# A recurrence and a mixture of experts on one core: head order, a rounded bias pass, gate transposes moved, last chunk cut 384+128

## Chip, cores and metric

One core of a Trainium2 chip. The metric is the device time of one execution in microseconds; before the change three runs gave 110.6 (median), 109.71 and 113.1.

## What is computed

From the reference, cut to what matters (x is 32 x 32 x 128, that is 32 sequences of T=32 steps; H = I = 128, E = 16 experts, K = 4 chosen):

```python
xw = einsum('ntd,dh->nth', x, Wx) + b
h_t = tanh(xw_t + h_{t-1} @ Wh)                      # scan over T
xn = h * rsqrt(mean(h*h, -1) + EPS) * norm_scale     # 1024 tokens
logits = xn @ wg + bg
vals, idx = top_k(logits, 4);  gates = softmax(vals) # spread to gate_full [token, 16]
hh = einsum('th,ehd->etd', xn, w1) + b1
a = minimum(hh[..., ::2], 7);  g = clip(hh[..., 1::2], -7, 7)
s = a * sigmoid(1.702 * a) * (g + 1)
y = einsum('eti,eih->eth', s, w2) + b2
out = x + h + einsum('eth,te->th', y, gate_full)
```

Every expert is computed for every token; the gate matrix is zero where an expert wasn't chosen. The term of b2 is therefore one matmul per token block, gates (16 per token) times b2 (16 x 128).

## The kernel before

Everything lies transposed: features on the 128 partitions, tokens as columns, 8 tiles of 128 tokens (a tile is four steps of the recurrence, 32 sequences wide). The tokens go in three chunks of 2, 2 and 4 tiles. A **unit** is 512 columns of up, activation and down work: two experts of a 2-tile chunk, or one expert of the 4-tile chunk. So chunk 0 is units 0 to 7, chunk 1 units 8 to 15, chunk 2 units 16 to 31.

The order of each engine's instructions is written out by hand, and engines meet at semaphores. The loop variable `v` counts units:

- **PE** (lines 821 to 881). First the *head*: five dummy matmuls of 512 columns on constants (`keep_warm`), then the eight steps of tiles 0 and 1. Behind steps 0, 1, 2, 4 and 6 stand two dummies of 256 columns each, behind the others useful small work; behind step 7 the rstd transpose of tile 0 (`lay_rstd(0)`), `x_wx(2)` and one more dummy. Then sums of squares of tile 1, raw logits of tiles 0 and 1, `lay_rstd(1)`, `x_wx(3, 2)`. Then units: `up` for half a (psA) and half b (psB), each as three passes in rounded fp32 (high·high, low·high, high·low; L774), one recurrence step in either slot, and `down(v - 4)` in plain fp32 (L804). An fp32 matmul shows in the trace as two instructions, a rounded one as one.
- **ACT**: relu (L483) and the gated activation (L492) of each unit in place in PSUM, tanh (L441), the high parts of w1 (L449), squares (L454), and `copy_gates` (L458). It is a queue in order: what stands behind a wait waits too.
- **DVE**: `lin` (L667), `act` (L682), norm and routing of each pair of tiles (q = 0 to 3), ending with the scale of the gates (L609).
- **POOL**: low parts of w1, powers, and the product with the gates (L406) two units behind.
- **SP**: weight loads, and for each pair the gates to DRAM and back as columns broadcast over partitions (L314, L320).

The gates of pair q are transposed by PE in unit v = 1, 7, 11 and 15 (`GATES_T`), ahead of `down(v - 4)`; ACT copies the 16 rows to `gT`. The bias of b2 starts each chunk's sum in PSUM: one fp32 matmul with 16 rows of weights per bank (L796) ahead of the first down of the chunk. The last chunk's sum lies in two banks, 256 columns in psR and 256 in psM. At the end the last four units' downs are issued bank by bank (`down_half`), each bank followed by a DVE add and a store.

## Time and profile before

| | |
|---|---|
| three runs | 110.6 us median (109.71 to 113.1) |
| the profiled execution | 110.22 us, of which the span is 108.4 us |
| busy, share of the span | PE 95%, DVE 60%, POOL 59%, ACT 56% |
| matmul instructions on PE | 562 |

The span goes from the first to the last instruction. Times in the rows are microseconds from the span's start unless a row says otherwise. In the chain view each piece is the start, the length and the work on the path that ended last. In the timeline a row may merge instructions (`x6`), and a bracket tells how long the engine was idle before it and what ended that. A matmul's record includes the time in which its last columns drain, so records overlap; the spacing of starts tells the rate.

### The profile page before, as it was taken

What the parts mean: (1) busy time and instruction counts of PE and PEld (TensorE: products, weight loads), DVE (VectorE), ACT (ScalarE), POOL (GpSimd) and SP (SyncE); (2) the same over time, 40 slices, a digit from 0 to 9 for tenths busy, and PEclk for the clock granted to TensorE, in tenths of its full rate; (3) what the DMA queues carried; (4) which work ended last, traced back from release to release, by engine and by line L of the source; (5) the groups of instructions that cost most, each with busy time, mean ns of one, the idle gap of its engine ahead of it and who ended that gap; (6) DMA issues with size and microseconds to landing.
All of it is one profiled execution on the core that took longest, in us unless ns stands there. A gap on an engine that the chain in (4) does not pass through costs nothing.

```text
span 108.4 us, 1718 instructions
## 1 busy us (share of the span) xinstructions
PE 102.9 (95%) x562; PEld 87.0 (80%) x562; DVE 64.6 (60%) x173; ACT 60.8 (56%) x139; POOL 63.8 (59%) x76
## 2 busy tenths in 40 slices
PE   7899999999999999999999969999999999999980
PEld 2557689988899999999989958886888888888760
DVE  0101367876818976399747996578266656666730
ACT  5144826899646486767716645665364566645400
POOL 3004348987791996449980799896444466545400
PEclk9999999999999999999999999999999999999999
DMA  2997930007930002991058814991000000000012
GB/s 77 235 335 266 398 113 0 0 6 234 390 159 3 0 0 74 296 379 39 12 165 246 308 60 116 336 361 59 6 0 0 0 3 0 0 0 0 0 48 48
DMA packets 4936, 12.94 MB, mean 119 GB/s; under 512 B 752, under 2 KB 1728, under 8 KB 4928
## 3 DMA queue, kind: packets, MB, share of 16 engines
q1 hardware_dynamic: 4704, 12.67, 34.7%
q10 hardware_dynamic: 224, 0.17, 0.6%
q8 instruction: 4, 0.07, 0.2%
q14 instruction: 4, 0.03, 0.1%
HBM read 12.25 MB, written 0.59 MB: 118 GB/s over the span
## 4 chain that ended last, share of the span: by engine, by line
PE 79%; DVE 9%; ACT 5%; DMA 2%; issue 1%; DVEq 0%
PE psA L774 19%; PE psB L774 17%; PE psY L804 10%; PE psR L804 5%; PE psR L722 5%; PE psM L804 5%; PE psY L722 2%; DMA wx_x_sb<-in_wx_x 2%; PE psA L751 2%; PE psM L729 2%; PE psR L714 2%; ACT psA L483 2%; PE psR L816 2%; ACT psA L492 2%; PE psM L816 2%; DVE lin L667 1%
## 5 line engine op out<-in xcount | busy, mean ns | idle before, releaser
L406 POOL TENSOR_TENSOR actg<-act,gate_cols 128x512 f32<-128x512 f32 x31 | 39.4, 1279 | 13.7 <-DVE act L682 12.9
L667 DVE TENSOR_SCALAR lin<-psB,one_b1b 128x256 f32<-128x256 f32 (+1 forms) x48 | 26.0, 569 | 23.3 <-PE psB L774 23.3
L483 ACT ACTIVATE psA<-psA,lim_b1a 128x256 f32<-128x256 f32 (+1 forms) x48 | 23.8, 515 | 26.5 <-PE psA L774 26.5
L682 DVE SCALAR_TENSOR_TENSOR act<-lin,psA 128x512 f32<-128x512 f32 x32 | 21.9, 686 | 1.8 <-ACT psA L492 0.5
L492 ACT ACTIVATE psA<-psA,limit_col 128x512 f32<-128x512 f32 x32 | 21.1, 660 | 0.8
L774 PE MATMUL psA<-xn_hi,w_hi 128*128 128x256 f32 (+1 forms) x48 | 20.5, 428 | 0.0
L804 PE MATMUL psY<-actg,w_sb 128*128 128x256 f32 x64 | 17.1, 389 | 0.0
L774 PE MATMUL psB<-xn_hi,w_hi 128*128 128x256 f32 (+1 forms) x48 | 16.0, 332 | 0.0
L774 PE MATMUL psA<-xn_hi,w_lo 128*128 128x256 f32 (+1 forms) x48 | 15.8, 328 | 0.0
L774 PE MATMUL psB<-xn_lo,w_hi 128*128 128x256 f32 (+1 forms) x48 | 15.6, 325 | 0.0
L774 PE MATMUL psB<-xn_hi,w_lo 128*128 128x256 f32 (+1 forms) x48 | 15.5, 323 | 0.0
L774 PE MATMUL psA<-xn_lo,w_hi 128*128 128x256 f32 (+1 forms) x48 | 15.5, 327 | 0.0
L389 POOL TENSOR_TENSOR w_lo<-w_sb,w_hi 128x256 fp32r<-128x256 f32 x13 | 9.2, 733 | 8.2 <-ACT w_hi L449 8.2
L804 PEld LDWEIGHTS psY<-actg,w_sb 128*128 128x128 f32 x64 | 11.2, 190 | 1.9 <-POOL actg L406 0.3
L368 POOL TENSOR_TENSOR expo<-euler,diff 128x6 f32<-128x6 f32 x4 | 5.3, 1326 | 10.4 <-DVE diff L577 10.4
L441 ACT ACTIVATE small_h<-psR,small_h 128x32 f32<-128x32 f32 x24 | 6.9, 286 | 7.6 <-PE psR L722 7.3
L722 PEld LDWEIGHTS psR<-small_h 128*128 128x128 f32 x48 | 8.8, 210 | 2.7 <-ACT small_h L441 1.9
L774 PEld LDWEIGHTS psA<-xn_hi,w_hi 128*128 128x128 f32 x48 | 9.6, 201 | 0.8 <-issue 0.4
L774 PEld LDWEIGHTS psA<-xn_hi,w_lo 128*128 128x128 f32 x48 | 9.7, 202 | 0.5
L774 PEld LDWEIGHTS psA<-xn_lo,w_hi 128*128 128x128 f32 x48 | 9.5, 200 | 0.7
L774 PEld LDWEIGHTS psB<-xn_hi,w_lo 128*128 128x128 f32 x48 | 9.4, 195 | 0.7
L774 PEld LDWEIGHTS psB<-xn_lo,w_hi 128*128 128x128 f32 x48 | 9.4, 195 | 0.7
(82 smaller groups left out, 136.0 us busy)
## 6 DMA issues: line engine op xcount, KB each, us to landing
gate_cols<-gate_rows SPq DMA_DIRECT2D x16, 512.0 KB, 6.0
w_sb<-in_w SPq DMA_DIRECT2D x4, 512.0 KB, 8.0
w_sb<-in_w SPq DMA_DIRECT2D x4, 256.0 KB, 9.3
out<-yT SPq DMA_DIRECT2D x3, 128.0 KB, 1.7
wx_x_sb<-in_wx_x SPq DMA_DIRECT2D x1, 320.0 KB, 6.0
wx_x_sb<-in_wx_x SPq DMA_DIRECT2D x2, 128.0 KB, 2.5
small_h<-in_small ACTq DMA_DIRECT2D x1, 105.0 KB, 2.7
gate_rows<-gT SPq DMA_DIRECT2D x4, 16.0 KB, 1.4
```

The lines of the kernel that those rows point to most:

```text
L368: nc.gpsimd.tensor_tensor(expo[:, tq, 1:K], euler[:, :, :], diff[:, tq, 1:K], ALU.pow).then_inc(pool_chain, 1)
L389: nc.gpsimd.tensor_tensor(w1_lo[:, pe_, a, :], w1_sb[:, pe_, a, :], w1_hi[:, pe_, a, :].bitcast(F32), ALU.subtract).then_inc(w1_half_ready, 1)
L406: nc.gpsimd.tensor_tensor(by_pair(actg[:, u % SUM_DEPTH, w]), by_pair(act[:, u % ACT_DEPTH, w]), gate_block(u, w), ALU.mult).then_inc(actg ...
L441: nc.scalar.activation(hT[:, (t + 1) * N:(t + 2) * N], step_psum(t), ACT.Tanh, bias=b_col[:, 0:1]).then_inc(step_done, 1)
L483: last = nc.scalar.activation(psA[u % 2][:, o], psA[u % 2][:, o], ACT.Relu, scale=-1.0, bias=lim_b1a[:, e0 + k:e0 + k + 1])
L492: nc.scalar.activation(psA[u % 2][:, 0:w], psA[u % 2][:, 0:w], ACT.Gelu_apprx_sigmoid, scale=-1.0, bias=limit_col[:, :]).then_inc(swish_do ...
L667: last = nc.vector.tensor_scalar(lin[:, v % 2, o], psB[v % 2][:, o], one_b1b[:, e0 + k:e0 + k + 1], LIMIT + 1.0, ALU.add, ALU.min)
L682: nc.vector.scalar_tensor_tensor(act[:, v % ACT_DEPTH, 0:w], lin[:, v % 2, 0:w], 1.0 - LIMIT, psA[v % 2][:, 0:w], ALU.max, ALU.mult).then_ ...
L722: nc.tensor.matmul(step_psum(t), wh_sb, hT[:, t * N:(t + 1) * N], start=False, stop=True, skip_group_check=True).then_inc(step_mm, 1)
L774: last = nc.tensor.matmul(bank[:, part(c, k)], w[:, e0 + k, a, :], x_part[:, cols(c)], start=((k, m) in first), stop=((k, m) in end))
L804: last = nc.tensor.matmul(y, w2_sb[:, e0 + k, :], actg[:, u % SUM_DEPTH, a], start=False, stop=(e0 + k == E - 1))
L816: ins = nc.tensor.matmul(y_end_bank(k)[:, 0:PW], w2_sb[:, e0, :], actg[:, u % SUM_DEPTH, o], start=False, stop=(u == NU - 1))
```

## The change

1. **Head of PE.** The two dummies behind step 6 and the one behind step 7 go. Raw logits of tile 0 are computed behind step 6, those of tile 1 directly behind the sums of tile 1. `x_wx(3, 2)` is cut in two: tile 3 ahead of `lay_rstd(1)`, tile 4 behind it.
2. **b2 and the gates in rounded fp32.** b2 comes from the host five times over (80 x 128); DVE rounds it and makes the last 16 rows the low part (`b2_parts`). The scale of the gates writes three copies with 16 zero columns between them (96 wide), so that the transpose gives 80 rows; ACT copies these, rounded, to `gS` besides the 16 fp32 rows of `gT`, and DVE replaces rows 32 to 47 by the low part (`gates_low`). The bias matmul is one rounded pass over 80 rows of weights instead of an fp32 matmul over 16. b2 is loaded on ACT's queue behind `small` instead of last on SP's.
3. **Gate transposes** stand behind `down(v - 4)` in units 7, 11 and 15.
4. **Last chunk** lies in the banks as 384 + 128 columns; stores and the final adds follow.

```diff
-                if t in (0, 1, 2, TL, TL + 2):
-                    keep_warm(2)
+                if t in (0, 1, 2, TL):
+                    keep_warm(2, WARM // 2)
...
+                elif t == TL + 2:
+                    pe.wait_ge(wg_ready, 1)
+                    raw_logits(range(0, 1), psB[0])
+                elif t == HEAD - 1:
                     lay_rstd(0)
                     x_wx(2, 1)
-            keep_warm(1)
+            sums(1).then_inc(m_mm, 1)
+            raw_logits(range(1, 2), psB[0]).then_inc(raw_mm, 1)
             pe.wait_ge(step_done, HEAD)
-            sums(1).then_inc(m_mm, 1)
-            pe.wait_ge(wg_ready, 1)
-            raw_logits(pair_tiles(0), psB[0]).then_inc(raw_mm, 1)
+            x_wx(3, 1)
             lay_rstd(1)
-            x_wx(3, 2)
+            x_wx(4, 1, start=False)
...
-                nc.scalar.activation(gT[:, q * PW:(q + 1) * PW], psX[0:E, 0:PW], ACT.Copy).then_inc(gT_ready, 1)
+                nc.scalar.activation(gT[:, qc], psX[0:E, 0:PW], ACT.Copy).then_inc(gT_ready, 1)
+                nc.scalar.activation(gS[:, qc], psX[0:GR, 0:PW], ACT.Copy).then_inc(gS_high, 1)
...
+            def gates_low(q):
+
+                dve.wait_ge(gS_high, q + 1)
+                low, qc = slice(LOW_AT, LOW_AT + E), slice(q * PW, (q + 1) * PW)
+                nc.vector.tensor_tensor(gS[low, qc], psX[low, 0:PW], gS[low, qc].bitcast(F32),
+                                        ALU.subtract).then_inc(gS_ready, 1)
...
+            def b2_parts():
+
+                dve.wait_ge(b2_loaded, 16)
+                mark(nc.vector.tensor_copy(b2_w[:, :], b2_sb[:, :]))
+                settled()
+                low = slice(GR - E, GR)
+                nc.vector.tensor_tensor(b2_w[low, :], b2_sb[low, :], b2_w[low, :].bitcast(F32),
+                                        ALU.subtract).then_inc(b2_ready, 1)
...
+            b2_parts()
             stats(0)
...
                     for o, y in y_parts(c):
-                        nc.tensor.matmul(y, b2_sb[:, :], gT[:, cols(c)][:, o], start=True, stop=False)
+                        nc.tensor.matmul(y, b2_w[:, :], gS[:, cols(c)][:, o], start=True, stop=False)
...
+            o = [slice(0, 3 * P), slice(3 * P, W)][k]
+            return o, (psM if k else psR)[:, 0:o.stop - o.start]
...
                 if v >= LAG:
                     down(v - LAG)
+                    for q in at(GATES_T, v):
+                        transpose_gates(q)
```

PE's instructions behind step 6 (L722 before, L753 after), up to the first up matmul (L774, L806); L751 is a dummy, L729/L760 a sum of squares, L735/L767 raw logits, L744/L776 the rstd transpose, L714/L745 x·Wx. Before:

```order
L722 MATMUL psR<-small_h 128x32
L751 MATMUL psA<-const-bfloat16-1.0 128x256 x2
L722 MATMUL psR<-small_h 128x32
L744 MATMUL psM<-ident,rstd 128x128
L714 MATMUL psY<-wx_x_sb 128x128
L751 MATMUL psA<-const-bfloat16-1.0 128x256
L729 MATMUL psM<-ones,sq 128x1
L735 MATMUL psB<-wg_scaled,small_h 128x16 x2
L744 MATMUL psM<-ident,rstd 128x128
L714 MATMUL psR<-wx_x_sb 128x256
L774 MATMUL psA<-xn_hi,w_hi 128x256
```

After:

```order
L753 MATMUL psR<-small_h 128x32
L767 MATMUL psB<-wg_scaled,small_h 128x16
L753 MATMUL psR<-small_h 128x32
L776 MATMUL psM<-ident,rstd 128x128
L745 MATMUL psY<-wx_x_sb 128x128
L760 MATMUL psM<-ones,sq 128x1
L767 MATMUL psB<-wg_scaled,small_h 128x16
L745 MATMUL psR<-wx_x_sb 128x128
L776 MATMUL psM<-ident,rstd 128x128
L745 MATMUL psR<-wx_x_sb 128x128
L806 MATMUL psA<-xn_hi,w_hi 128x256
```

Three dummies are gone, one raw-logits matmul moved ahead of step 7, and half of the x·Wx that stood between the rstd transpose and the first up now stands ahead of that transpose.

PE in unit 15, from its last up matmul to the first of unit 16 (L758/L790 transposes of the gates, L804/L836 the down), with what each waits for. Before:

```order
L774 MATMUL psB<-xn_lo,w_hi 128x256
L758 MATMUL psX<-ident,gates 16x128 [waits gT_ready,scale_done]
L758 MATMUL psX<-ident,gates 16x128
L804 MATMUL psY<-actg,w_sb 128x256 [waits actg_done]
L804 MATMUL psY<-actg,w_sb 128x256
L774 MATMUL psA<-xn_hi,w_hi 128x512 [waits act_done,xn_hi_ready]
```

After:

```order
L806 MATMUL psB<-xn_lo,w_hi 128x256
L836 MATMUL psY<-actg,w_sb 128x256 [waits actg_done]
L836 MATMUL psY<-actg,w_sb 128x256
L790 MATMUL psX<-ident,gates_w 80x128 [waits gS_ready,scale_done]
L790 MATMUL psX<-ident,gates_w 80x128
L806 MATMUL psA<-xn_hi,w_hi 128x512 [waits act_done,xn_hi_ready]
```

The down now stands ahead of the wait for the scale. The same holds in units 7 and 11.

ACT around the copy of the first pair's gates in unit 1 (L441/L450 tanh, L449/L458 high parts of w1, L483/L494 relu). Before:

```order
L441 ACTIVATE small_h<-psY,small_h 128x32
L458 ACTIVATE gT<-psX 16x256
L449 ACTIVATE w_hi<-w_sb 128x2x128 x2
L483 ACTIVATE psA<-psA,lim_b1a 128x256
L441 ACTIVATE small_h<-psR,small_h 128x32
```

After:

```order
L450 ACTIVATE small_h<-psY,small_h 128x32
L468 ACTIVATE gT<-psX 16x256
L469 ACTIVATE gS<-psX 80x256
L458 ACTIVATE w_hi<-w_sb 128x2x128 x2
L494 ACTIVATE psA<-psA,lim_b1a 128x256
L450 ACTIVATE small_h<-psR,small_h 128x32
```

One copy more stands between two tanh of the recurrence.

## Rows read from the trace of the kernel before

**Rows 1.** Page: busy time and share of the span; relu's group of instructions

```profile
PE 102.9 (95%) x562; PEld 87.0 (80%) x562; DVE 64.6 (60%) x173; ACT 60.8 (56%) x139; POOL 63.8 (59%) x76
...
L483 ACT ACTIVATE psA<-psA,lim_b1a 128x256 f32<-128x256 f32 (+1 forms) x48 | 23.8, 515 | 26.5 <-PE psA L774 26.5
```

**Rows 2.** Chain in order of time (start, us, what); last row: PE's timeline

```profile
14.69 0.85 PE psR L714 x2
15.54 1.30 PE psA L774 x6
...
31.46 0.72 PE psB L774 x6
...
19.84 0.34 PE L774 MATMUL psA<-xn_lo,w_hi 128*128 128x256 f32 x1
```

**Rows 3.** Chain, where it leaves PE for ACT in units 1 and 2

```profile
22.11 0.24 ACT gT L458
...
23.28 0.22 ACT small_h L441
...
23.54 0.41 PE psR L722 x2
```

**Rows 4.** Timeline of DVE, rounded norm of tile 1

```profile
14.73 0.35 DVE L538 SCALAR_TENSOR_TENSOR xn_hi<-small_h,psM 128x128 fp32r<-128x128 f32 x1 [0.30 <-PE psM L744]
```

**Rows 5.** Chain, bias matmuls (L796) and downs (L804) of chunks 0 and 2

```profile
28.84 0.62 PE psY L796 x2
29.46 1.06 PE psY L804 x4
...
32.32 0.95 PE psY L804 x4
...
74.85 0.62 PE psR L796 x2
...
75.91 0.63 PE psR L804 x2
...
78.35 0.43 PE psR L804 x2
```

**Rows 6.** Timelines of POOL, DVE, PE and the weight loads

```profile
27.87 2.49 POOL L406 TENSOR_TENSOR actg<-act,gate_cols 128x512 f32<-128x512 f32 x2 [0.76 <-DMA gate_cols<-gate_rows]
...
50.78 0.10 PEld L758 LDWEIGHTS psX<-ident,gates 128*16 128x16 f32 x2 [0.16 <-DVE gates L609]
...
62.85 0.33 DVE L609 TENSOR_TENSOR gates<-gate_sum,inv 128x32 f32<-128x32 f32 x1
63.10 0.67 DVE L682 SCALAR_TENSOR_TENSOR act<-lin,psA 128x512 f32<-128x512 f32 x1
...
63.23 0.39 PE L758 MATMUL psX<-ident,gates 128*16 128x128 f32 x2 [0.84 <-DVE gates L609]
```

**Rows 7.** The end: chain, and DVE's timeline for the gate product

```profile
64.48 0.68 PE psA L774 x3
...
101.64 1.86 PE psR L816 x8
103.49 1.74 PE psM L816 x8
105.26 0.42 DVE yT L701
...
102.31 0.76 DVE L695 TENSOR_TENSOR actg<-act,gate_cols 128x256 f32<-128x256 f32 x2
```

**Rows 8.** DMA issues by line (KB each, us to landing); timelines of ACT's queue, DVE

```profile
small_h<-in_small ACTq DMA_DIRECT2D x1, 105.0 KB, 2.7
...
bg_sb<-in_bg SPq DMA_DIRECT2D x1, 8.0 KB, 8.0
...
0.74 0.40 ACTq L435 DMA_DIRECT2D small_h<-in_small  x1
...
10.10 0.16 DVE L521 TENSOR_SCALAR meansq<-psM 128x1 f32<-128x1 f32 x1 [6.22 <-PE psM L729]
```

More of the change, by code:

```diff
@@ L43, in adaln_rnn_moe_kernel @@
     NU = UNIT0[NC]
-    WARM, WARM_START, WARM_GAP = 512, 5, 256
+    WARM, WARM_START = 512, 5
     LAG = 4
@@ L69, in adaln_rnn_moe_kernel @@
     EQ = E // GATE_GROUPS
+    GR = 5 * E
+    LOW_AT = 32
     ctx = ExitStack()
@@ L128, in adaln_rnn_moe_kernel @@
         gate_sum = sb("gate_sum", [P, NT, E])
-        gates = sb("gates", [P, NT, E])
+        gates_w = sb("gates_w", [P, NT, 6 * E])
         gT = sb("gT", [E, NT * P])
+        gS = sb("gS", [GR, NT * P], F32R)
         gate_rows = nc.dram_tensor("gate_rows", [NQ, E, PW], F32)
@@ L176, in adaln_rnn_moe_kernel @@
         gT_ready = sem("gT_ready")
+        gS_high = sem("gS_high")
+        gS_ready = sem("gS_ready")
+        b2_ready = sem("b2_ready")
         a_mm = sem("a_mm")
@@ L235, in pieces, with y_end @@
             return [slice(0, h), slice(h, W)] if u == NU - 1 else [slice(0, width(u))]
-        def y_end_bank(k):
-            return psM if k else psR
+        def y_end(k):
+            o = [slice(0, 3 * P), slice(3 * P, W)][k]
+            return o, (psM if k else psR)[:, 0:o.stop - o.start]
         def gate_block(u, o):
@@ L503, in _ @@
             acte.wait_ge(yT_ready, NC + 1)
-            store(acte, slice((NT - 2) * P, NT * P), slice(P // 2, P))
+            store(acte, slice((NT - 1) * P, NT * P), slice(P // 2, P))
         @block.vector
@@ L669, in _ @@
                     last.then_inc(lin_done, 1)
+                for q in at(GATES_T, v - 1):
+                    gates_low(q)
                 for q in at(STATS, v):
@@ L698, in _ @@
             for k in range(2):
-                dve.wait_ge(y_end, k + 1)
-                o = slice((NT - 4 + 2 * k) * P, (NT - 2 + 2 * k) * P)
-                nc.vector.tensor_tensor(yT[:, o], xT[:, o], y_end_bank(k)[:, 0:PW],
-                                        ALU.add).then_inc(yT_ready, 1)
+                dve.wait_ge(y_done, k + 1)
+                o, y = y_end(k)
+                o = slice((NT - 4) * P + o.start, (NT - 4) * P + o.stop)
+                nc.vector.tensor_tensor(yT[:, o], xT[:, o], y, ALU.add).then_inc(yT_ready, 1)
         @block.tensor
@@ L709, in turn, with x_wx @@
                     pe.wait_ge(m_read, psM_turn(what) - 1)
-            def x_wx(j, n):
+            def x_wx(j, n, start=True):
                 pe.wait_ge(x_loaded if j > 2 else x1_loaded if j else wx_x0_loaded, 16)
-                nc.tensor.matmul(xw_cols(j, n), wx_sb, xT[:, j * P:(j + n) * P], start=True, stop=True,
+                nc.tensor.matmul(xw_cols(j, n), wx_sb, xT[:, j * P:(j + n) * P], start=start, stop=True,
                                  skip_group_check=True)
@@ L732, in raw_logits @@
             def raw_logits(ts, bank):
-                for k, j in enumerate(ts):
+                for j in ts:
+                    k = j % 2
                     last = nc.tensor.matmul(bank[:, 16 + k * E:16 + (k + 1) * E], hT[:, N + j * P:N + (j + 1) * P],
@@ L755, in transpose_gates @@
                 if q:
-                    pe.wait_ge(gT_ready, q)
+                    pe.wait_ge(gS_ready, q)
                 for k, j in enumerate(pair_tiles(q)):
-                    last = nc.tensor.transpose(psX[0:E, k * P:(k + 1) * P], gates[:, j, :], ident[:, :])
+                    last = nc.tensor.transpose(psX[0:GR, k * P:(k + 1) * P], gates_w[:, j, 0:GR], ident[:, :])
                 last.then_inc(gates_mm, 1)
@@ L781, in y_parts @@
                     return [(slice(0, CHUNKS[c] * P), psY[:, 0:CHUNKS[c] * P])]
-                return [(slice(k * PW, (k + 1) * PW), y_end_bank(k)[:, 0:PW]) for k in range(2)]
+                return [y_end(k) for k in range(2)]
             def down(u):
@@ L864, in _ @@
                         step(t)
-                for q in at(GATES_T, v):
-                    transpose_gates(q)
+                if v < LAG:
+                    for q in at(GATES_T, v):
+                        transpose_gates(q)
                 for q in at(STATS, v):
@@ L871, in _ @@
                     down(v - LAG)
+                    for q in at(GATES_T, v):
+                        transpose_gates(q)
                 for t in steps_at(v, 1):
@@ L901 @@
         "w2": f["ffn_w2"].transpose(1, 0, 2),
-        "b2": f["ffn_b2"],
+        "b2": _np.tile(f["ffn_b2"], (5, 1)),
     }
```

33 lines of the change are left out of this document (18 added, 15 removed).

## The prediction

> **What bounds the kernel now.** First the page's busy shares: PE is busy 102.9 of the 108.4 us span, 95% [rows 1]. A busy PE can still be one that waits inside its queue, so the second view is the chain that ended last, in order of time. It runs through PE nearly everywhere from 15.54 us to the end. There the reader is to see what one six-matmul half of a unit costs: 1.30 us in the first unit and 0.72 at 31.46 [rows 2]. Six passes in 1.30 us are 0.217 us for 256 columns, TensorE's lower level (1.2 GHz); six in 0.72 are 0.12, the upper one (2.4 GHz). The page's clock row shows nothing of this; the spacing of the matmuls does, and the matmul at 19.84 is the first with a shorter record, 0.34 instead of 0.41 [rows 2]. The chain leaves PE at three places: in the second unit, where ACT's queue is full and PE's recurrence step waits for a tanh [rows 3]; and twice where the gates come from DVE and the transposes wait for them [rows 6]. Behind the last matmul stand one DVE add and a store [rows 7]. So a microsecond saved on PE counts, except ahead of those places.
>
> The sum is made against the profiled execution, 110.22 us (span 108.4 and 1.8 around it). It lies 0.4 us under the median of the three runs, 110.6, which themselves lie between 109.71 and 113.1. About 2% (2.2 us) is what a measurement of this kernel can tell from no change.
>
> **1. The head.** Dummies go from behind step 6 and from behind step 7; one raw-logits tile takes the first place, and x·Wx of tile 3 moves ahead of the rstd transpose. PE at 14.69 issues x·Wx of tiles 3 and 4 as 2 x 256 columns, 0.85 us, and the first up matmul comes at 15.54 [rows 2]. With 128 columns left there it costs half, 0.43, and ends at 15.12. But xn_hi of tile 1 ends at 14.73+0.35 = 15.08 [rows 4], and a stalled weight load has still to run. Row 23.54 shows such a start: a step that was waited for costs 0.41 [rows 3] where a flowing one costs 0.14 (two matmuls of 32 columns), so 0.27 is latency. Then the up stream starts at about 15.08+0.04+0.27 = 15.4. Gain 0.1 (0 to 0.3). That the piece moved forward costs nothing: half of the raw logits left that place (0.44 of the 0.88), it takes 0.43. The removed dummies were not waited for.
>
> **2. ACT's second copy of the gates.** copy_gates now issues 80x256 behind 16x256. For q=0 this stands in the chain: the copy takes 0.24 there, then come the w1 copies and relu, then the tanh at 23.28 which PE's step at 23.54 waits for [rows 3]. A second copy of as many columns costs another 0.24, say +0.25 (0.2 to 0.35; partitions work in parallel). For q=1 to 3 ACT has slack: over the span it idles 26.5 us before relu waiting for PE [rows 1]; there it costs nothing unless that idle is not where the copy is.
>
> **3. b2 as one rounded pass.** Before, each bias matmul is fp32, two instructions. In chunk 0 it adds a piece of 0.62, and the down behind it takes 1.06 instead of 0.95 in the next unit [rows 5]: 0.62+1.06-0.95 = 0.73. In chunk 2 it is 0.62 and 0.63 and, behind each, a second piece that takes 0.43 like the one at 78.35: 2.11, against two such pieces, 0.86, for a unit without it: 1.25 [rows 5]. Pure streaming is 0.217 a pass, so 0.43 and 0.87; the rest, 0.30 and 0.38, is start-up around the 16-row weights. After, a rounded 256-column pass is 0.12 [rows 2], and 384+128 columns are 0.24. No row shows a weight block of 80 rows. If the start-up goes wholly, chunks 0 and 1 gain 0.73-0.12 = 0.6 each and chunk 2 gains 1.0; if it stays as it is, 0.3, 0.3 and 0.63. I take the second, since 80 rows are like the 16 a partly filled array, and the nearest row is the bias matmul itself.
>
> Chunk 0's gain has a lid: down(0) needs POOL's first gate product, and POOL started the pair at 27.87 behind the gate columns' DMA, 2.49 for two [rows 6], so the first is there at 29.12, and the down can't begin before 29.17 against 29.46 now. With +0.25 from part 2 and -0.1 from part 1 PE comes 0.15 late and wins 0.3: net of parts 1 to 3 up to unit 4 is **-0.15** (0 to -0.3). Chunk 1: **-0.3** (to -0.6). Chunk 2: **-0.65** (to -1.0).
>
> DVE rounds the low part of each pair (gates_low). Nearest row: an add of 128x256 from PSUM, 0.42 [rows 7]; it stands at v=2, 8, 12 and 16 behind lin. At v=2 DVE then waits for ACT anyway; at the others PE asks for act two units later. Zero, at most 0.1 in all. The scale writes 96 instead of 32 elements: 0.33 now [rows 6], +0.07 by the ratio of 16 to 48 columns against rows of that size, an estimate (0 to 0.15), and it lies in the two waits of part 4. b2_parts puts two DVE instructions and a wait for b2's load ahead of stats(0). DVE idles 6.22 us before that one at 10.10 [rows 8], so the two (some 0.6) are free if b2 lands by 9.4. Its DMA is issued by ACT behind small_h's, near 1.2 us. Nearest rows: small_h itself 2.7 us to landing, bg behind the weights on SP's queue 8.0 [rows 8]: it lands between 4 and 9.7. I take the early side since the same queue has only small_h ahead; late side +0.3. The page "DMA: Bandwidth & Descriptors" of the Trainium skill (HWDGE ordering) says that SP and ACT each own one ring on each of the same 16 DMA engines. By that b2 is not queued behind SP's weights but shares the engines with them; it moves no term, and no row here shows an ACT DMA issued among SP's weights other than small_h.
>
> **4. Transposes behind the down.** At v=15 the transposes start at 63.23 after 0.84 us in which PE only waited for the scale that ends at 63.18 [rows 6]. Now the down (0.87) runs in that hole. What is late next is unit 16, which needs DVE's act(14): it stands behind the scale, at 63.10, takes 0.67 [rows 6], and ends at 63.77, with the wider scale at 63.84. A stalled start adds 0.27, so unit 16 streams from 64.1 instead of 64.48 [rows 7]: **-0.35** (-0.2 to -0.6), not 0.84. At v=11 PE's wait is 0.16 to 0.2 [rows 6] and act(10) is early: **-0.2** (0 to -0.2). At v=7 there is no wait. The gates of v=15 leave PE no later than now, since the down fits the hole; at v=7 and 11 they leave some 0.6 later, but ACT takes them only behind the tanh of the step that follows the down, and that is later still. q=0, whose columns set the lid in chunk 0, was not moved.
>
> **5. The tail.** The last chunk is cut 384+128 instead of 256+256. The columns of a unit stay the same, and so does its time. Now psR takes 1.86 and psM 1.74, the first with a stall for the DVE product that ends at 103.07 in two halves [rows 7]: three 384-wide ones last 3 x 0.65 (0.43 x 384/256) from 101.64, to 103.6, so the wait for both halves is covered; then 0.64 and 4 x 0.22: 105.1 instead of 103.49+1.74 = 105.23. The add behind shrinks from 0.42 [rows 7] to about 0.28, and the last store is half as large (between 0 and -0.1). **-0.25** (0 to -0.4).
>
> Sum: -0.15 -0.2 -0.3 -0.35 -0.65 -0.25 = **-1.9**, from 110.2: **108.3 us** (1.7% less). With every term at its small end (nothing for the head, v=11 and the tail, 0.2 for v=15) 109.1, at its large end 107.1.
>
> **Rivals.** *A. The start-up around the bias goes with the 16-row weights and the fp32 pairs.* For it: a six-pass half at 0.72 has none [rows 2]. Against: those are full 128 rows. Chunks 1 and 2 give 0.3+0.35 more: 107.7. *B. The savings on PE are eaten by ACT and DVE.* The chain leaves PE only twice behind unit 4, so it takes new DVE work (four scales, four gates_low, at 0.07 and 0.42) in the queue between lin and act: if the c1 gain and the v=15 gain vanish, 109.0. Against: DVE is idle before most lins. *C, the other side: the clock rises later.* This execution went up at 19.84 after some 4 us of up matmuls without a hole, the steps with dummies before it having stayed at the low level [rows 2]. After the change PE does less between steps 6 and 8. Each half of a unit at the low level costs 1.30 against 0.72, 1.2 us a unit; ACT's full queue hides some 0.2 of it in units 2 and 3, so 1.0 a unit. One more unit low: 109.3; from two more on the gain is used up, and with three (up to unit 4) it is 111.3, slower than before. For it: the spread of the runs, 3.4 us, is as large as three units. Against: all of the dense stretch, and the step pattern up to step 5, stays, and the rise did not come from the removed dummies in the profile. The page "TensorE: Matmul & The Clock Gate" of the Trainium skill ("The HAM clock gate") says the observation of activity is free-running, so the point of the rise varies from run to run; by that the removal would cost only in some executions. The spread agrees, though no row shows its cause. *D. It doesn't do what it says:* if the rounded pass with K=80 costs as much as the pair did, part 3 falls out and parts 1, 2, 4 and 5 leave +0.15-0.2-0.35-0.25: 109.6.
>
> **Chances.** Forecast 50% (own range 107.9 to 108.9), A 18%, B 10%, C with one unit 8%, C with more 8%, D 6%. Against the median of 110.6, 2% less is 108.4: half of the forecast and nearly all of A lie under it, 0.45. Slower by over 2% (over 112.8) is only the far part of C, 0.07. The rest, 0.48, is within 2%. The range leaves out the low tenth beyond A and most of C's slow half: 106.9 to 110.4.
>
> **What would show it.** In the changed profile: the bias pieces of the chain at about 0.4 in chunk 0 and 1 and 0.6 in chunk 2 in place of 0.73 and 1.25 (0.12 and 0.24: A). The second copy at some 0.25 on ACT near 22.3, and PE's step behind it as late as now. Transposes at v=15 with no DVE wait, and instead PE waiting for act in front of unit 16. First up matmul near 15.4, and the spacing of matmuls falling to 0.12 at 19 to 21 us; if it falls at 23 or later, C. DVE's stats(0) at 10.1; later means b2 landed late. Wrong I am if the chain behind unit 4 passes ACT or DVE at new places, or if the time moves by over 3 us in either direction, which no term here can do.

## The result, and the profile after the change

| | median of all runs | lowest to highest | runs |
|---|---|---|---|
| before | 109.96 us | 109.24 to 113.1 | 15 |
| after | 108.27 us | 107.55 to 111.62 | 15 |

The ratio is 0.984, with a 95% interval from 0.981 to 0.988: 1.6% less, a real gain, but under 2%. The ratio is taken without the runs that were over 1.5% above the fastest of their kernel. The forecast was 108.3. It was right as a sum, and by luck: the steps behind it were not all right, and two misses of 0.7 to 0.8 us cancelled, which is shown term by term below.

The profiled execution of the changed kernel took 110.58 us. The gate rows of the first pair took 2.94 us to DRAM in it, where ten of the fourteen profiles of all kernels have 1.4, so its times from unit 4 on are read here as differences only.

From the page of after, to set beside [rows 1]; the columns are the same:

```profile
PE 100.8 (93%) x557; PEld 84.4 (78%) x557; DVE 67.3 (62%) x179; ACT 61.6 (57%) x143; POOL 64.7 (59%) x77
...
L494 ACT ACTIVATE psA<-psA,lim_b1a 128x256 f32<-128x256 f32 (+1 forms) x48 | 23.7, 513 | 23.5 <-PE psA L806 23.4
```

PE has 2.1 us less busy time, and each other engine some more than before. Relu's idle time shrank from 26.5 to 23.5.

From the chain of after in order of time, to set beside [rows 5]; the bias matmul is now L828, the down L836:

```profile
56.70 0.22 PE psY L828
56.91 0.86 PE psY L836 x4
...
76.48 0.18 PE psR L828
76.66 0.06 PE psM L828
76.72 0.69 PE psR L836 x2
77.42 0.22 PE psM L836 x2
```

In chunk 2 the bias and the downs behind it take 1.15 us where they took 2.11. The down of chunk 1 behind its bias takes 0.86, no more than a down alone: not only the streaming of the fp32 pair went, its start-up went too.

Spans can't be compared directly, since a wait for the first gates moves everything behind it. So the kernels are compared unit by unit: on PE's timeline, the start of the first `psA` up matmul of one unit to that of the next. For unit 12 these rows are, in before (3.81 us):

```profile
52.01 0.37 PE L774 MATMUL psA<-xn_hi,w_hi 128*128 128x256 f32 x1
...
55.82 0.47 PE L774 MATMUL psA<-xn_hi,w_hi 128*128 128x256 f32 x1
```

and in after (3.20 us):

```profile
54.23 0.37 PE L806 MATMUL psA<-xn_hi,w_hi 128*128 128x256 f32 x1
...
57.43 0.47 PE L806 MATMUL psA<-xn_hi,w_hi 128*128 128x256 f32 x1
```

All units in which kernels differ by over 0.03 us, in us ("end" is from the start of unit 31 to the end of the span; the experiments' names are explained below):

| unit | what the change touches there | before | after | u_bias | u_head | swap | k16 | g8 |
|---|---|---|---|---|---|---|---|---|
| 1 | (the clock rises here) | 2.68 | 2.52 | 2.35 | 2.24 | 2.77 | 2.59 | 2.46 |
| 2 | ACT's second copy | 2.48 | 2.74 | 2.48 | 2.75 | 2.73 | 2.74 | 2.74 |
| 4 | bias of chunk 0, first gates | 4.35 | 5.71 | 6.04 | 3.78 | 4.39 | 4.04 | 3.75 |
| 5 | | 2.91 | 2.91 | 4.47 | 2.90 | 2.89 | 2.90 | 2.90 |
| 7 | transposes | 2.87 | 2.95 | 2.96 | 2.96 | 3.07 | 2.96 | 2.96 |
| 11 | transposes | 3.09 | 3.13 | 3.13 | 3.13 | 3.20 | 3.13 | 3.13 |
| 12 | bias of chunk 1 | 3.81 | 3.20 | 3.81 | 3.21 | 3.23 | 3.50 | 3.21 |
| 15+16 | transposes | 5.76 | 5.80 | 5.83 | 5.82 | 6.20 | 5.83 | 5.84 |
| 20 | bias of chunk 2 | 3.48 | 2.64 | 3.59 | 2.64 | 2.64 | 2.96 | 2.65 |
| end | last downs, store | 9.35 | 8.92 | 8.92 | 8.94 | 8.92 | 8.89 | 8.86 |

Units 12 and 20 and the end gain, and unit 4 does where the first gates come in time; unit 2 and the units with transposes lose. The units not listed differ by 0.03 at most (unit 0 of u_bias, where the clock rose early, by 0.11).

Unit 2 of u_bias is as short as before's although ACT's second copy is in it: the early clock moved the start of that unit. PE's wait for the tanh behind the copy tells the copy's cost in every profile: 0.19 us in before and 0.18 in g8_late, where the copy stands elsewhere, and 0.36 (u_bias) to 0.45 in eleven profiles that have it there.

Units 4 and 5 show what late gates cost. In four profiles (after, u_bias, b2_only, nodummy) the first gate rows took 2.8 to 3.3 us to DRAM instead of 1.4, and PE then stood 1.60 to 1.91 us ahead of the first down. In three of them the granted clock fell to 0.50, TensorE's 1.2 GHz level, behind that wait, and unit 5 took 4.47 (u_bias), 4.80 (b2_only) and 4.84 (nodummy) instead of 2.90. These are the executions of 113.2, 113.37 and 113.28 us. In after PE waited 1.70 and the clock stayed up. From nodummy, PE's timeline and the page's row of the granted clock (40 slices of 2.8 us, in tenths):

```profile
31.21 2.07 PE L836 MATMUL psY<-actg,w_sb 128*128 128x256 f32 x4 [1.91 <-POOL actg L414]
...
PEclk9999999999955799999999999999999999999999
```

Why the gate rows come late in some executions is open.

### The profile page after: what moved, and what is told of

Its sections match the earlier page's. It is cut to its first block, busy times and chain, and to the rows that moved or that the text cites. A ratio compares the mean times of both kernels' runs of the same rounds, so it can differ in the third digit from the quotient of the medians.

```text
span 108.8 us, 1720 instructions
## 1 busy us (share of the span) xinstructions
PE 100.8 (93%) x557; PEld 84.4 (78%) x557; DVE 67.3 (62%) x179; ACT 61.6 (57%) x143; POOL 64.7 (59%) x77
## 4 chain that ended last, share of the span: by engine, by line
PE 73%; DMA 12%; ACT 4%; POOL 3%; DVE 2%; issue 2%; SPq 1%; POOLq 0%; DVEq 0%
PE psA L806 19%; PE psB L806 17%; PE psY L836 12%; PE psR L836 7%; DMA w_sb<-in_w 6%; PE psR L753 4%; DMA gate_cols<-gate_rows 4%; DMA gate_rows<-gT 3%; PE psM L836 2%; PE psR L848 2%; POOL actg L414 2%; PE psM L760 2%; PE psR L745 2%; ACT psA L494 1%; ACT psA L503 1%
## 5 line engine op out<-in xcount | busy, mean ns | idle before, releaser
L494 ACT ACTIVATE psA<-psA,lim_b1a 128x256 f32<-128x256 f32 (+1 forms) x48 | 23.7, 513 | 23.5 <-PE psA L806 23.4
L836 PE MATMUL psY<-actg,w_sb 128*128 128x256 f32 x64 | 17.2, 391 | 2.5 <-POOL actg L414 2.5
L806 PE MATMUL psA<-xn_hi,w_hi 128*128 128x256 f32 (+1 forms) x48 | 19.2, 400 | 0.1
L806 PE MATMUL psB<-xn_hi,w_hi 128*128 128x256 f32 (+1 forms) x48 | 16.0, 334 | 0.0
L806 PE MATMUL psA<-xn_hi,w_lo 128*128 128x256 f32 (+1 forms) x48 | 15.6, 325 | 0.0
L806 PE MATMUL psB<-xn_lo,w_hi 128*128 128x256 f32 (+1 forms) x48 | 15.6, 324 | 0.0
L806 PE MATMUL psB<-xn_hi,w_lo 128*128 128x256 f32 (+1 forms) x48 | 15.5, 323 | 0.0
L806 PE MATMUL psA<-xn_lo,w_hi 128*128 128x256 f32 (+1 forms) x48 | 15.5, 326 | 0.0
L836 PEld LDWEIGHTS psY<-actg,w_sb 128*128 128x128 f32 x64 | 11.2, 190 | 4.2 <-POOL actg L414 2.9
L450 ACT ACTIVATE small_h<-psR,small_h 128x32 f32<-128x32 f32 x24 | 6.8, 285 | 9.0 <-PE psR L753 8.8
L753 PEld LDWEIGHTS psR<-small_h 128*128 128x128 f32 x48 | 8.6, 210 | 3.1 <-ACT small_h L450 2.2
L376 POOL TENSOR_TENSOR expo<-euler,diff 128x6 f32<-128x6 f32 x4 | 5.3, 1324 | 9.1 <-DVE diff L588 9.1
L806 PEld LDWEIGHTS psA<-xn_hi,w_hi 128*128 128x128 f32 x48 | 9.7, 202 | 0.5 <-issue 0.4
L806 PEld LDWEIGHTS psB<-xn_lo,w_hi 128*128 128x128 f32 x48 | 9.4, 195 | 0.7
L806 PEld LDWEIGHTS psB<-xn_hi,w_lo 128*128 128x128 f32 x48 | 9.4, 196 | 0.7
L753 PE MATMUL psR<-small_h 128*128 128x32 f32 x48 | 9.0, 272 | 0.9 <-ACT small_h L450 0.9
L806 PEld LDWEIGHTS psA<-xn_lo,w_hi 128*128 128x128 f32 x48 | 9.3, 197 | 0.7
```

The source lines that it names most:

```text
L376: nc.gpsimd.tensor_tensor(expo[:, tq, 1:K], euler[:, :, :], diff[:, tq, 1:K], ALU.pow).then_inc(pool_chain, 1)
L450: nc.scalar.activation(hT[:, (t + 1) * N:(t + 2) * N], step_psum(t), ACT.Tanh, bias=b_col[:, 0:1]).then_inc(step_done, 1)
L494: last = nc.scalar.activation(psA[u % 2][:, o], psA[u % 2][:, o], ACT.Relu, scale=-1.0, bias=lim_b1a[:, e0 + k:e0 + k + 1])
L753: nc.tensor.matmul(step_psum(t), wh_sb, hT[:, t * N:(t + 1) * N], start=False, stop=True, skip_group_check=True).then_inc(step_mm, 1)
L806: last = nc.tensor.matmul(bank[:, part(c, k)], w[:, e0 + k, a, :], x_part[:, cols(c)], start=((k, m) in first), stop=((k, m) in end))
L836: last = nc.tensor.matmul(y, w2_sb[:, e0 + k, :], actg[:, u % SUM_DEPTH, a], start=False, stop=(e0 + k == E - 1))
```

## The experiments

### Four parts undone, one at a time

**u_bias** is the changed kernel with PE's bias matmul as before; all that ACT and DVE do for the rounded pass stays.

```diff
-                        nc.tensor.matmul(y, b2_w[:, :], gS[:, cols(c)][:, o], start=True, stop=False)
+                        nc.tensor.matmul(y, b2_sb[0:E, :], gT[:, cols(c)][:, o], start=True, stop=False)
```

> The changed kernel with only PE's bias matmul as before (fp32, 16 rows of b2, gates from gT); ACT's second copy, gates_low and b2_parts stay, their results unused. As predicted (start-up around the bias stays in the rounded form): 0.3+0.3+0.65 us slower than the changed kernel, about 109.5. Rival A (start-up goes with the pair): 0.6 in chunk 1 and 1.0 in chunk 2, and up to 0.3 in chunk 0, 1.6 to 1.9 slower, about 110.0. In the trace of the changed kernel the bias and the down behind it take 1.08 instead of 1.68 in chunk 1, which speaks for A. Chain pieces of the bias here: 0.62 with 1.06 behind.

Measured: 110.35 us median (109.35 to 113.2), ratio to before 1.003 (0.999 to 1.007). That is past rival A's 110.0 and far from the forecast's 109.5: the whole gain of the change is gone. Units 12 and 20 are back at 3.81 and 3.59, so the rounded pass is worth 0.61 and 0.95 there with this split of the banks.

**u_transp** puts the transposes of units 7, 11 and 15 ahead of the down again.

```diff
-                if v < LAG:
-                    for q in at(GATES_T, v):
-                        transpose_gates(q)
+                for q in at(GATES_T, v):
+                    transpose_gates(q)
...
                     down(v - LAG)
-                    for q in at(GATES_T, v):
-                        transpose_gates(q)
```

> The changed kernel with the gate transposes ahead of the down again in units 7, 11 and 15. As predicted the move gave 0.2+0.35: 0.55 slower than the changed kernel, 108.8. Rival E, from the trace after: the down now waits in the same hole for POOL's gate product of unit 11, which stands in POOL's queue behind the powers of the last pair (0.79 us of PE idle before the down at 64.79), so one wait only took the place of the other: 0 to 0.2 slower, 108.3 to 108.5.

Measured: 108.89 us (107.91 to 110.05), ratio 0.987 (0.980 to 0.995). Its interval overlaps with the changed kernel's; by the units the move is worth 0.06 at unit 11 (3.19 against 3.13) and 0.07 at 15 and 16 (5.87 against 5.80).

**u_head** has the head of before, dummies included (the first part of the diff above, reversed).

> The changed kernel with the head's order and its three dummies of before (the rest of the change stays). As predicted: 0.1 slower than the changed kernel, 108.4. Rival C (dummies hold the clock up in some executions): as fast or faster than the changed kernel, with the matmul spacing falling from 0.21 to 0.12 earlier.

Measured: 108.09 us (107.71 to 108.87), ratio 0.985 (0.979 to 0.990). The head's order gives nothing that can be seen: from the rounded norm of tile 0 (`xn_hi`) to the first up matmul it is 3.21 us in after and in u_head and 3.20 in before.

**u_tail** cuts the last chunk 256 + 256 again.

```diff
-            o = [slice(0, 3 * P), slice(3 * P, W)][k]
+            o = [slice(0, 2 * P), slice(2 * P, W)][k]
...
-                    pe.wait_ge(actg_tail, 2)
+                    pe.wait_ge(actg_tail, k + 1)
```

> The changed kernel with the last chunk cut 256+256 and its stores as before. As predicted: 0.25 slower, 108.5. If the first of the two rivals for the end holds, that the store's landing decides whatever its size and the larger first store is late, then no difference (108.3) and in the trace the last landing belongs to the first store of the pair.

Measured: 108.69 us (107.42 to 109.28), ratio 0.986 (0.978 to 0.994). The end takes 9.34 instead of 8.92, so the tail's cut is worth 0.42, and the rival by which the store alone decides falls. But unit 20 is at 2.48 instead of 2.64: the same cut costs 0.16 there, in the unit with the bias. Why is open; later units take the same 2.25 with either cut.

**b2_only** undoes head, transposes and tail together and keeps the rounded pass.

> The changed kernel with the head, the transposes and the tail of before: only the rounded bias is left of the change. Theory from the unit tables: the bias gives 0.6 in unit 12, 0.85 in unit 20 and up to 0.3 in unit 4, the head nothing, the transposes 0.1, the tail 0.4, and ACT's second copy takes 0.25. So 0.5 slower than the changed kernel, 108.8, and 1.2 faster than the kernel before. By the recorded sum it would be 0.9 slower than the changed kernel, 109.2.

Measured: 109.24 us (107.92 to 113.37), ratio 0.987 (0.981 to 0.994), with units 12 and 20 at 3.20 and 2.48. By the ratios it is 0.3 us slower than the changed kernel, nearer to the 0.5 from the units than to the 0.9 of the recorded sum, though the intervals of the two kernels overlap. Part 2 alone gives most of what the change gives.

### Where the start-up around the bias went

**k16** keeps the rounded pass but gives it 16 rows instead of 80.

```diff
-                        nc.tensor.matmul(y, b2_w[:, :], gS[:, cols(c)][:, o], start=True, stop=False)
+                        nc.tensor.matmul(y, b2_w[0:E, :], gS[0:E, cols(c)][:, o], start=True, stop=False)
```

> The changed kernel with the rounded bias pass over 16 rows (the high parts of gates and b2 only, which leaves out the low parts of the bias). If the start-up of before belonged to the partly filled array (16 rows of weights), the piece of the bias in chunk 1 grows again from 0.22 towards 0.12+0.19 = 0.3 and the down behind it from 0.86 to 1.06. If it belonged to the fp32 pair, the pieces stay 0.22 and 0.86 and unit 20 stays 2.64.

**fp80** does the opposite, an fp32 pair over 80 rows.

```diff
-        gS = sb("gS", [GR, NT * P], F32R)
+        gS = sb("gS", [GR, NT * P])
...
-                        nc.tensor.matmul(y, b2_w[:, :], gS[:, cols(c)][:, o], start=True, stop=False)
+                        nc.tensor.matmul(y, b2_sb[:, :], gS[:, cols(c)][:, o], start=True, stop=False)
```

> The changed kernel with the bias matmul in fp32 (two instructions a matmul) over the same 80 rows; the bias is then added twice, since b2 stands five times and one of the three gate copies is zeroed. The run k16 showed the start-up back with 16 rows of rounded weights (0.31 and 1.06). If the number of rows decides and not the fp32 pair, the start-up stays small here: 0.43+0.1 and 0.86 in chunk 1, unit 12 at 3.5 and unit 20 at 3.0 to 3.1. If the pair has a start-up of its own, unit 12 is 3.8 and unit 20 is 3.5, as before.

One execution each: 109.55 and 109.48 us. The chain at the bias of chunk 1, in k16:

```profile
54.95 0.31 PE psY L828
55.26 1.06 PE psY L836 x4
```

and in fp80:

```profile
54.63 0.53 PE psY L828 x2
55.16 0.86 PE psY L836 x4
```

With 16 rows the down behind takes 1.06, as in before; with 80 rows 0.86, even behind an fp32 pair. Unit 12 takes 3.81 with fp32 and 16 rows, 3.50 with rounded and 16, 3.51 with fp32 and 80, 3.20 with both. The two effects add: 0.30 us for the start-up around weights of 16 rows, 0.31 for the pass. Unit 20 says the same: 3.59 (u_bias), 2.96 (k16), 3.22 (fp80) and 2.64 (after) are 0.32 to 0.37 for the rows and 0.58 to 0.63 for the passes. The 3.22 misses the 3.0 to 3.1 that was expected of fp80: the fp32 pairs over both banks cost more than was reckoned.

The timelines of the weight loads show where the 0.30 goes. In after:

```profile
56.52 0.19 PEld L828 LDWEIGHTS psY<-gS,b_w 80*128 80x128 f32 x1
56.63 0.74 PEld L836 LDWEIGHTS psY<-actg,w_sb 128*128 128x128 f32 x4
```

and in k16:

```profile
54.88 0.18 PEld L828 LDWEIGHTS psY<-gS,b_w 16*128 16x128 f32 x1
55.19 0.73 PEld L836 LDWEIGHTS psY<-actg,w_sb 128*128 128x128 f32 x4
```

The load of the bias's weights itself takes 0.19 and 0.18. But in after the down's weights begin to load 0.08 us behind the start of the bias matmul (56.55), while it streams, and in k16 0.31 behind it (54.88). With 16 rows the next load no longer hides behind the matmul. Why the number of rows does that is not shown. The Trainium skill, page "TensorE: Matmul & The Clock Gate" (section "Step-by-step: what each phase is for"), says of a weight load that its time goes by the columns and that the row count doesn't matter. The two durations agree; what a change from 128 rows to 16 and back costs the stream is 0.30 us here and isn't covered by it.

### POOL and DVE at the gates of the last pair

**swap** issues POOL's gate product ahead of the powers of the rstd step.

```diff
+                if v >= POOL_LAG:
+                    gate_product(v - POOL_LAG)
                 for q in at(RSTD, v):
                     power_expo(q)
                     place_expo(q)
-                if v >= POOL_LAG:
-                    gate_product(v - POOL_LAG)
```

> The changed kernel with one edit on POOL: in units 5, 9 and 13 the gate product stands ahead of the two powers of the pair's routing instead of behind them. If the down of units 11 and 15 waits for exactly that product (E), PE's wait before the down in unit 15 (0.79 us) goes, units 15 and 16 together fall from 5.80 us by 0.3 or more towards the bound set by act(14), and the whole is 0.3 to 0.5 faster than the changed kernel, 107.8 to 108.0. If the wait belongs to DVE's late gates, nothing changes, or the powers start later and it is 0.1 to 0.3 slower.

Measured: 109.38 us (108.34 to 113.74), ratio 0.992 (0.988 to 0.997), where the changed kernel has 0.984 (0.981 to 0.988): slower, not faster, though the intervals just touch, and by the units 0.40 slower at 15 and 16. That the down only needs its product earlier fell as a theory. The timelines of POOL, DVE and PE in swap show what was late instead:

```profile
62.55 2.51 POOL L414 TENSOR_TENSOR actg<-act,gate_cols 128x512 f32<-128x512 f32 x2
...
62.65 0.17 DVE L615 RECIPROCAL inv<-den 128x2 f32<-128x2 f32 x1
62.85 1.07 DVE L620 TENSOR_TENSOR gates_w<-gate_sum,inv 128x96 f32<-128x96 f32 x1
63.84 0.68 DVE L713 SCALAR_TENSOR_TENSOR act<-lin,psA 128x512 f32<-128x512 f32 x1
...
64.67 0.47 PE L806 MATMUL psA<-xn_hi,w_hi 128*128 128x512 f32 x1 [0.27 <-DVE act L713]
```

The scale of 96 elements takes 1.07 us here and 0.40 in the changed kernel. It begins 0.30 us after POOL's next product and ends as that product does (63.82 on the chain). `act` stands behind it, and unit 16 behind `act`.

The Trainium skill, page "SBUF — State Buffer" (section "SBUF: two separate sides"), states that DVE and GpSimd share a pair of ports as an exclusive lock, taken for a whole instruction, by a DVE operation with two SBUF inputs among others (against a GpSimd instruction that reads SBUF); the loser waits in full. The runs agree for the scale: in before, after, swap and g8 the scale of pairs 1 to 3 starts inside a POOL product and ends 0.04 to 0.12 us behind it. The expectation of swap_ts below calls 0.26 its time alone. That is the scale of pair 0, which starts as one of POOL's low-part instructions ends, so 0.26 is a scale that hardly had to wait. The reductions and the reciprocal ahead of the scale, with one SBUF input, run inside the same product in 0.27, 0.15 and 0.17 (after). But not every POOL instruction that reads SBUF holds such a DVE instruction up, though by the rule it would: `hot` (L601), with two inputs in SBUF, takes 0.29 in the middle of POOL's 1.32 us power of six columns (L376), in after and in swap.

**swap_ts** was to avoid that, on top of swap's edit, with one SBUF tensor per instruction and one instruction per tile.

```diff
-                nc.vector.tensor_tensor(
-                    gates_w[:, ts, :].rearrange("p j (a b e) -> p j a b e", a=3, b=2)[:, :, :, 0, :],
...
+                for j in pair_tiles(q):
+                    last = nc.vector.tensor_scalar(
+                        gates_w[:, j, :].rearrange("p (a b e) -> p a b e", a=3, b=2)[:, :, 0, :],
+                        gate_sum[:, j, :].rearrange("p (a e) -> p a e", a=1).to_broadcast([P, 3, E]),
+                        inv[:, j:j + 1], None, ALU.mult)
```

> The run swap with the scale of the gates as two DVE instructions that read one SBUF tensor and a per-partition scalar, in place of one that reads two SBUF tensors. In all traces the scale of pairs 1 to 3 ends 0.04 to 0.1 us after POOL's gate product, which is 0.26 alone, 0.4 in the changed kernel and 1.07 in swap. If two SBUF inputs of a DVE instruction wait for POOL's to end, the scale here takes 0.2 to 0.3 a piece, act(14) starts 0.5 us earlier, and units 15 and 16 together fall from 6.20 to 5.5 or 5.6, under the 5.76 of the kernel before. If the block is on any DVE access while POOL multiplies, they stay at 6.2.

Measured: 112.81 us in one execution, far on the wrong side. Its timelines of POOL and DVE:

```profile
64.82 2.48 POOL L414 TENSOR_TENSOR actg<-act,gate_cols 128x512 f32<-128x512 f32 x2
...
65.13 2.22 DVE L621 TENSOR_SCALAR gates_w<-gate_sum,inv 128x48 f32<-128x48 f32 x2
```

The two instructions end with POOL's two products: 2.22 us for 96 elements. One SBUF input doesn't keep this instruction clear of POOL. The same page (section "Who interferes with whom") counts `tensor_scalar` among the operations that can take the pair in a two-port mode; this row agrees with that, where the expectation had left it out. Units 11 and 15 take 4.34 and 5.19.

### The lid on unit 4

**g8** brings the gate columns of a pair in eight DMAs of 256 KB instead of four of 512.

```diff
-    GATE_GROUPS = 4
+    GATE_GROUPS = 8
```

> The changed kernel with the gate columns of each pair spread by eight DMAs of 256 KB instead of four of 512 KB. In the traces unit 4 is what varies most between executions (3.78 to 5.71 us in the changed kernel and its kin, 4.35 in the kernel before), because POOL's first product waits for the first of these DMAs. If the size of that first DMA counts, it lands about 1 us earlier, unit 4 falls to what PE needs (3.5), and the whole is 0.3 to 1.0 faster than the changed kernel: 107.3 to 108.0. If a fixed delay of the DMA or traffic of the weights decides, no difference; the doubled number of issues on SP could cost up to 0.3.

Measured: 107.63 us (107.07 to 109.18), ratio to before 0.977 (0.971 to 0.984), the best median of all kernels here. Its interval overlaps with the changed kernel's (0.981 to 0.988), so the gain over it is likely rather than shown. In g8 POOL starts its first products without a wait, and PE without one behind them; POOL's timeline and the chain:

```profile
26.28 0.64 POOL L404 TENSOR_TENSOR wx_x_sb<-wx_x_sb,small_h 128x256 f32<-128x256 f32 x1
26.95 2.51 POOL L414 TENSOR_TENSOR actg<-act,gate_cols 128x512 f32<-128x512 f32 x2
...
28.66 0.21 PE psY L828
28.87 0.86 PE psY L836 x4
```

In u_head, with four DMAs, POOL still waits 0.40 for the columns:

```profile
27.25 2.50 POOL L414 TENSOR_TENSOR actg<-act,gate_cols 128x512 f32<-128x512 f32 x2 [0.40 <-DMA gate_cols<-gate_rows]
```

Unit 4 takes 3.75 in g8 and from 3.78 (u_head) to 4.93 (swap_ts) in the profiles with four DMAs whose gate rows took 1.4 us. The first of the column DMAs takes 3.4 us from issue to landing in g8 and 3.7 in g8_late, and 3.8 to 5.0 in the profiles with four. u_head shows that four DMAs can be as good: with 3.8 for the first, unit 4 is only 0.03 longer than in g8. In after and u_bias it takes 5.71 and 6.04; the chain of after stands there for both transfers of the first pair's gates:

```profile
22.83 2.94 DMA gate_rows<-gT
...
25.79 4.25 DMA gate_cols<-gate_rows
```

**g8_late** also moves ACT's second copy of the first pair from unit 1 to unit 3, behind relu.

```diff
                 nc.scalar.activation(gT[:, qc], psX[0:E, 0:PW], ACT.Copy).then_inc(gT_ready, 1)
-                nc.scalar.activation(gS[:, qc], psX[0:GR, 0:PW], ACT.Copy).then_inc(gS_high, 1)
+                if q:
+                    copy_high(q)
...
+                if u == 3:
+                    copy_high(0)
```

> The changed kernel with two edits: the gate columns by eight DMAs (the run g8, 0.9774 of the kernel before), and for the first pair ACT's second copy (gS) moved from unit 1 to unit 3, behind relu, with DVE's gates_low one unit later. If the copy in unit 1 is what lifted unit 2 from 2.48 to 2.74 us, unit 2 is back at 2.5 here, nothing else moves, and the whole is 0.2 to 0.3 faster than g8: 107.3 to 107.5, ratio 0.975. If DVE's act(3) comes late behind the moved gates_low, unit 4 or 5 takes the 0.25 back and the time is that of g8 (107.6) or more.

Measured: 107.98 us (106.99 to 108.6), ratio 0.977 (0.971 to 0.982), not to be told from g8. Unit 2 is back at 2.49, and unit 4 gives 0.15 of the 0.25 back (3.90). The size of the DMAs had not taken the lid off for good: POOL waits 0.52 for the columns here, its first product starting at 28.02. Seen from the start of unit 0 (16.00 here, 14.98 in g8) that is 12.02, against 11.97 in g8.

### The clock

**nodummy** takes away the dummies that the changed head still has between its steps.

```diff
-                if t in (0, 1, 2, TL):
-                    keep_warm(2, WARM // 2)
-                elif t == 3:
+                if t == 3:
```

> The changed kernel without the eight dummies between the steps of the head (the five at the start stay). Rival C says that dummies in the head hold up the activity from which the clock rises: without them the spacing of matmuls falls from 0.21 to 0.12 later than 19 to 20 us, at 1.0 us for each unit more, 109.3 or above. If only the dense stretch from 15 us on counts, the rise stays where it is and the time is that of the changed kernel, or 0.1 to 0.3 less where a dummy had delayed a step.

Measured: 108.65 us (107.72 to 113.28), ratio 0.984 (0.977 to 0.991): no different from the changed kernel within 0.7%. Its PE timeline where the spacing falls:

```profile
20.24 0.49 PE L806 MATMUL psB<-xn_hi,w_hi 128*128 128x256 f32 x1
20.57 0.29 PE L806 MATMUL psB<-xn_hi,w_lo 128*128 128x256 f32 x1
20.69 0.28 PE L806 MATMUL psB<-xn_lo,w_hi 128*128 128x256 f32 x1
```

The matmul at 20.24 is the first with a shorter record (0.49; the first of a half before it has 0.56), and from 20.57 on they start 0.12 apart instead of 0.21. The first shorter record lies at 19.84 in before, 20.04 in after, 18.55 in u_head (the head of before) and 18.61 in u_bias (the changed head). It moves by 1.7 us between profiles, and by 1.5 between before, u_head and b2_only (20.03), which have one and the same head. So the three dummies of the change don't decide it. That all dummies together do nothing is not shown by one profile: nodummy's is the latest of all.

## Why the prediction was right, and where it wasn't

The sum of -1.9 us stands against -1.7 between the medians. It was taken from a profile of 110.2; from the median of 109.96 it would have given 108.1, so the agreement of 108.3 with 108.27 to the last digit is chance. Term by term, by the units:

| term | predicted | measured | from |
|---|---|---|---|
| head | -0.1 | 0 | after against u_head, below |
| ACT's second copy | +0.25 | +0.26 | unit 2 |
| bias of chunk 0 | -0.3, with a lid | up to -0.6 | unit 4, g8 against before |
| bias of chunk 1 | -0.3 | -0.61 | unit 12 |
| bias of chunk 2 | -0.65 | -0.84 | unit 20; the split takes 0.16 of 1.0 |
| transposes, v=11 and 15 | -0.55 | +0.08 | units 11 and 15+16 |
| transposes, v=7 | 0 | +0.08 | unit 7 |
| tail | -0.25 | -0.43 | end |

The measured column adds up to -2.1 with unit 4 at its best; the medians hold runs in which the first gates are later. The bias was put 0.8 too small over the three chunks and the transposes 0.7 too large, and these two cancelled.

**Too small: the bias.** The step that failed is "if it stays as it is ... I take the second, since 80 rows are like the 16 a partly filled array". The forecast had worked out both ends, 0.3 and 0.6 for chunk 1, and the run landed on the far one to 0.01. So rival A was right in its mechanism and its price, as u_bias, k16 and fp80 show, and the total came out as forecast only because the terms of the transposes fell away. Its phrase "with the 16-row weights and the fp32 pairs" holds for the rows alone.

**Too large: the transposes.** The step that failed is "Now the down (0.87) runs in that hole". It doesn't: the down's own input was just as late. The chain of after at unit 15:

```profile
61.70 0.81 POOL expo L376
62.51 0.56 issue
...
63.11 0.16 POOL hot L384
...
63.46 1.28 POOL actg L414
64.74 0.04 issue
64.79 1.13 PE psY L836 x4
65.92 0.22 PE psX L790 x2
```

And this could have been read before the change. POOL's timeline of before has the product that this down needs:

```profile
61.86 1.27 POOL L406 TENSOR_TENSOR actg<-act,gate_cols 128x512 f32<-128x512 f32 x1
```

It ends at 63.13, the scale that the transposes waited for at 63.18 [rows 6]. The 0.84 us hole had two causes that ended 0.05 us apart, and the trace named the later. They are hardly independent: as swap showed, the scale doesn't end before the POOL product in which it starts. In before PE's wait in unit 15 ended at 63.23, 2.61 us into the unit; in after it ends 2.56 into it. At unit 11 it is the same: POOL's product of after ends at 52.84 and the down starts at 52.90. Against u_transp the move still gives 0.13. But u_transp takes 0.21 more than before in these units (3.19 and 5.87 against 3.09 and 5.76): its scale takes 0.40 instead of 0.33 [rows 6], and the transposes have 80 columns of weights. So the move only pays back part of what part 2 costs here.

**Nothing: the head.** The forecast took PE's start of the up stream, 15.54, from the chain, and let the two-tile x·Wx hold it. PE's timeline says otherwise. Before:

```profile
14.48 1.06 PE L714 MATMUL psR<-wx_x_sb 128*128 128x256 f32 x2
15.22 0.55 PE L774 MATMUL psA<-xn_hi,w_hi 128*128 128x256 f32 x1
15.58 0.41 PE L774 MATMUL psA<-xn_hi,w_lo 128*128 128x256 f32 x1
```

After (PE, then DVE's rounded norm of tile 1):

```profile
15.10 0.64 PE L745 MATMUL psR<-wx_x_sb 128*128 128x128 f32 x2
15.84 0.55 PE L806 MATMUL psA<-xn_hi,w_hi 128*128 128x256 f32 x1
...
15.35 0.35 DVE L549 SCALAR_TENSOR_TENSOR xn_hi<-small_h,psM 128x128 fp32r<-128x128 f32 x1 [0.73 <-PE psM L776]
```

The first up matmul begins 0.14 us after xn_hi of tile 1 ends in both: 15.22 against 14.73+0.35 = 15.08 [rows 4], and 15.84 against 15.70. x·Wx of two tiles was already hidden; the chain had counted the overlap of the records to it. The latency in the forecast was right, its base line was not. Seen from xn_hi of tile 0 the first six up matmuls end 4.83 us later both in after and in u_head. That this execution of after begins its first unit 0.62 us later than before's isn't the order: g8 and nodummy have the same order and begin at 14.98 and 15.12, u_head at 15.14. ACT waited 1.11 us for a weights' DMA at 8.00 in after, ahead of a tanh of the head, and 0.49 in u_head.

**Right.** ACT's copy (unit 2: +0.26; PE's wait for the tanh 0.44 instead of 0.19; in u_head's chain "ACT gS L469" is a piece of 0.26). The lid on chunk 0 by the first gate columns: where they are late, the gain isn't there, and in g8, where POOL doesn't wait, it is 0.6. b2's early side: the DMA landed after 2.9 us, DVE's two instructions ran at 4.06 and 4.32, and stats(0) still waited for PE, 6.11 us. `gates_low` cost 0.42 of DVE each and no time. The tail's sign, with a size of 0.43 just past its range of 0 to -0.4: psR takes 2.58 and psM 0.90 on the chain of after, 3.48 together against 3.60 [rows 7], and the add 0.29 instead of 0.42. Of the rest 0.09 lies behind the add (2.63 to the end of the span instead of 2.72) and 0.10 in unit 31 ahead of the last downs.

```profile
102.37 2.58 PE psR L848 x8
104.95 0.90 PE psM L848 x8
105.86 0.02 issue
105.88 0.29 DVE yT L733
```

**The other rivals.** B priced the loss at v=15 right in size and gave it to DVE's new work; it was POOL's product, and chunk 1's gain stayed. C, the later clock: after rose 0.2 us later than before, and before, u_head and b2_only spread as wide with one head. The spread of the runs, which C took as its support, has another source in the profiles kept: the three over 113 us are those in which the first gates came late and the clock fell back. D, that the rounded pass costs as much as the pair, fell with u_bias. Why the rise moves from profile to profile stays open.

## What to carry to other kernels

A wait in a profile names only the input that came last. Before an instruction is moved into the hole in front of another, look up when its own inputs are ready, on the timeline of the engine that makes them. A price bounded from two sides deserves a thought about which property makes it (here the rows of the weights, not the precision), since the ends were a factor of two apart. When a DVE instruction with two inputs in SBUF can fall beside a long POOL product, its place in time matters more than its size: 0.40 or 1.07 us for the same scale. And a wait of PE can cost more than its length, since the clock may fall behind it: 1.6 to 1.9 us of waiting cost up to 1.9 more in the next unit.

## What the runs showed of the hardware

- A bias matmul over 16 rows of weights costs 0.30 us more around it than one over 80 rows, rounded or in fp32, when 128-row matmuls stand on both sides (k16, fp80). The next weight load starts 0.31 us behind the start of the 16-row matmul, and 0.08 behind that of the 80-row one.
- The scale of the gates on DVE (two inputs in SBUF), started inside a POOL product, ends only as the product does: it took 0.40, 1.07 and, as two `tensor_scalar`, 2.22 us. A reduction or reciprocal with one input in SBUF wasn't held up (0.27, 0.15, 0.17), nor was `hot` with two inputs beside POOL's power (0.29). DVE's `lin`, which reads PSUM, took 0.86 and 0.87 for two in swap and in after, beside products or not.
- The first piece of the gate columns took 3.4 and 3.7 us to landing with 256 KB (g8, g8_late), and 3.8 to 5.0 with 512 KB (the other twelve profiles). POOL's first wait for it was gone in g8 and 0.52 in g8_late.
- Behind a wait of PE of 1.60, 1.62 and 1.91 us the granted clock fell to 0.50 (b2_only, u_bias, nodummy) and was back at 1.00 by 36 us in u_bias and by 38 us in the others; behind one of 1.70 it stayed at 1.00 (after).
- The point at which TensorE goes from its 1.2 to its 2.4 GHz spacing lay between 18.6 and 20.2 us in profiles whose first unit began at 15.0 to 16.0, and between 18.6 and 20.0 in the three with the head of before.
